# Attention block of 16 batches on one core: transposes two steps, value products six steps behind the scores

## The chip, the cores and the metric

One core of a Trainium2 chip. The time is the device time of one execution in microseconds; less is better. The program is written engine by engine: TensorE (matmuls and transposes into PSUM), VectorE, ScalarE, GpSimd, and a DMA queue issued by SyncE. The engines run their own instruction lists in order and meet only at semaphores.

## The reference, cut to what matters

```python
x = x + attn(xn) + ffn(xn)          # x: (16, 512, 128), xn = layernorm(x)

# attn, 16 heads of 64:
q = einsum('bse,hde->bhsd', xn, Wq) + bq ; k, v the same way
scores = q k^T / 8, causal (later keys masked)
att = softmax(scores) / 8
z = einsum('bhst,bhtd->bhsd', att, v) ; z.reshape(b, s, h * dh) @ proj

# ffn: base product, and of four low-rank experts the one that a router picks
base = xn @ W.T
lw = softmax(l2norm(xn @ Wp.T + bp) @ l2norm(sim) * scale)
res = top-1 weight * (xn @ Wd_e.T) @ Wu_e.T
```

## The kernel before

**Steps.** A batch is 32 steps: 8 pairs of heads times 4 blocks of 128 queries. Step s works on pair s // 4 and on query block s % 4, for both heads of the pair. Since the scores are causal, query block i needs i + 1 blocks of keys: 128, 256, 384 or 512 columns (`width`). The steps of all batches follow each other in one long row; a stage with a lag of n works, at step s, on the unit of step s - n (`due`).

**What a unit goes through.** TensorE makes the scores of both heads (`score`; for blocks 0 and 1 `narrow_scores`, both heads in one bank). VectorE adds the mask, scales and takes the row maximum (`maximum`, line 982). ScalarE takes the exponential and the row sum (`exponentials`, line 721). VectorE takes the reciprocals of the sums (`reciprocals`, line 971), one step late. GpSimd multiplies the probabilities by them (`normalise`, line 632). LAG_T = 3 steps behind the scores TensorE transposes the probabilities block by block (`transpose`, line 1297) into ptp; ScalarE copies head 0's, VectorE head 1's to pt (`evacuate_pt`, lines 732 and 994). Nine steps behind the first scores of a pair (LAG_PV) TensorE multiplies with the values, both heads (`values`, line 1323, 64 columns wide, 32 matmuls). ScalarE makes z_hi from the result one step later, VectorE z_lo = z - z_hi two steps later (`low_z`, line 1000). Eight pairs' results go through the output projection in quarters of six matmuls (`project`, line 1335) at the steps of LAG_OUT.

**Jobs.** Between the transposes and the values TensorE does one job of three 512-column matmuls in most steps (the table JOBS): the queries of a later pair at every step with s % 4 = 3, the keys at every one with s % 4 = 0, value blocks at V_STEPS, the router's product at 1, the transposed expert inputs (`gated`) at 17, the transposes of the next batch's normalised rows (`xt`) at 25. Jobs alternate between the banks jobp0 and jobp1, and a job waits until the job before it in its bank is read out. ScalarE makes the high part of a q or k job (and reads out v jobs), VectorE the low part (q_lo line 870, k_lo line 866); the list `evacuated(s)` says at which step. GpSimd copies k_lo twice to k_low (`pad_low_keys`, line 571) behind its products of the same step, SyncE moves q and k parts by DMA.

**Others.** The router runs in small VectorE instructions at STEP_SUMS to STEP_PARTS, with GpSimd's products (`usq`, `uprod`, at STEP_PRODUCTS) and a power at STEP_UNORM. The layer norm of the next batch is spread over the STEPS_STATS to STEP_SCALE steps. The base and low-rank matmuls stand at step 24, the sum's evacuation, transposes and final addition at 20 and 21.

## Time and profile before

| | us |
|---|---|
| median of 3 runs | 1348.27 (1347.8 to 1348.32) |
| the profiled execution | 1347.42 |
| its span | 1345.7 |
| TensorE matmuls busy | 1330.3 |
| TensorE weight loads busy | 1131.7 |
| VectorE busy | 1106.3 |
| ScalarE busy | 1085.9 |
| GpSimd busy | 997.7 |

The span is the time from the first to the last instruction of the core; the time of a run is that of the whole execution. Matmuls are pipelined, so that a matmul's row is longer than the distance to the next one: the distances between starts are what TensorE needs. Line numbers are those of the kernel before. From one batch to the next the same work starts 82.4 us later.

### The profile page before, as it was taken

Reading aid. Unit: us, or ns where it says so; the run is one execution under the profiler, and the core shown is the slowest. Engines: PE = TensorE matmul, PEld = TensorE weight load, DVE = VectorE, ACT = ScalarE, POOL = GpSimd, SP = SyncE. Lnnn points to the kernel's source line nnn. Section 1 sums busy time; section 2 is a strip of 40 time slices with the busy share of each in tenths; the row PEclk is TensorE's granted clock in tenths of the full one; section 3 lists DMA queues with packets and bytes.
Section 4 is the critical chain, followed back from the end, with each engine's and each line's share of the span. In section 5 each row is a group of like instructions: output and inputs, shape, how many; then the busy total and the mean of one; then the engine's idle time right before and its main releaser. Section 6 shows DMA issues by size and latency. Waiting matters only on the chain.

```text
span 1345.7 us, 34453 instructions
## 1 busy us (share of the span) xinstructions
PE 1330.3 (99%) x10783; PEld 1131.7 (84%) x10783; DVE 1106.3 (82%) x4001; ACT 1085.9 (81%) x3162; POOL 997.7 (74%) x1443
## 2 busy tenths in 40 slices
PE   7999999999999999999999999999999999999998
PEld 5788888888888888888888888888888888888887
DVE  8978888788787878878788787888878888788785
ACT  6887887888788887887888788788888887888785
POOL 7887777778777777777777768777677876778664
PEclk9999999999999999999999999999999999999999
DMA  6455444544544445454444544454454454545541
GB/s 155 95 119 118 103 112 113 122 104 111 125 107 116 105 113 123 103 122 110 116 103 115 123 103 115 112 122 110 103 124 113 103 122 112 122 95 119 118 103 48
DMA packets 112561, 150.59 MB, mean 112 GB/s; under 512 B 18239, under 2 KB 47230, under 8 KB 112382
## 3 DMA queue, kind: packets, MB, share of 16 engines
q1 hardware_dynamic: 111086, 147.97, 46.8%
q8 instruction: 90, 1.47, 0.5%
q14 instruction: 89, 0.73, 0.2%
q10 hardware_dynamic: 1296, 0.42, 0.2%
HBM read 10.69 MB, written 4.19 MB: 11 GB/s over the span
## 4 chain that ended last, share of the span: by engine, by line
PE 95%; ACT 1%; SPq 0%; POOL 0%; DVE 0%; DMA 0%; issue 0%; DVEq 0%; POOLq 0%
PE zp L1323 22%; PE ptp L1297 20%; PE jobp L1167 13%; PE scores L1285 9%; PE scores L1288 7%; PE outp L1335 7%; PE jobp L1172 6%; PE scores L1266 4%; PE scores L1263 3%; PE jobp L1182 1%; PE outp L1344 1%; PE jobp L1187 1%; PE jobp L1360 0%; PE jobp L1177 0%; ACT prob L721 0%; PE outp L1349 0%
## 5 line engine op out<-in xcount | busy, mean ns | idle before, releaser
L632 POOL TENSOR_TENSOR prob<-prob,rden 128x128 f32<-128x128 f32 (+3 forms) x1024 | 712.4, 720 | 247.2 <-DVE rden L971 240.7
L982 DVE CUSTOM_DVE_ANT_0 prob<-scores,mask 128x128 f32<-128x128 f32 (+3 forms) x1024 | 471.7, 488 | 199.8 <-issue 133.3
L721 ACT ACTIVATE prob<-prob,nmax 128x128 f32<-128x128 f32 (+3 forms) x1024 | 567.5, 559 | 12.1 <-DVE nmax L982 5.4
L1297 PE MATMUL ptp<-ident,prob 128*128 128x128 f32 x2560 | 366.9, 274 | 2.1 <-ACT pt L732 1.5
L1297 PEld LDWEIGHTS ptp<-ident,prob 128*128 128x128 f32 x2560 | 295.0, 140 | 27.4 <-POOL prob L632 5.0
L1323 PE MATMUL zp<-pt,v_sb 128*64 128x64 f32 (+3 forms) x4096 | 307.7, 303 | 0.0
L732 ACT ACTIVATE pt<-ptp 128x128 f32<-128x128 f32 (+3 forms) x512 | 221.2, 432 | 102.8 <-PE ptp L1297 102.8
L1323 PEld LDWEIGHTS zp<-pt,v_sb 128*64 128x64 f32 x4096 | 221.6, 137 | 51.2 <-issue 19.7
L994 DVE COPY pt<-ptp 128x128 f32<-128x128 f32 (+3 forms) x512 | 243.3, 475 | 3.9 <-PE ptp L1297 3.1
L571 POOL CAST k_low<-k_lo 64x512 fp32r<-64x512 f32 x256 | 156.0, 609 | 78.0 <-DVE k_lo L866 68.1
L1285 PE MATMUL scores<-k_twice,q_parts 128*128 128x384 f32 (+1 forms) x512 | 200.9, 392 | 0.0
L721 ACT ACTIVATION_READ_ACCUMULATOR prob<-prob,nmax 128x1 f32 x1024 | 198.3, 194 | 0.0
L1288 PE MATMUL scores<-k_low,q_parts 128*128 128x384 f32 (+1 forms) x512 | 186.8, 365 | 0.0
L710 ACT ACTIVATE z_hi<-zp 128x512 fp32r<-128x512 f32 x128 | 76.5, 598 | 127.4 <-PE zp L1323 125.4
L1285 PEld LDWEIGHTS scores<-k_twice,q_parts 128*128 128x128 f32 x512 | 95.9, 187 | 53.6 <-issue 42.7
L1288 PEld LDWEIGHTS scores<-k_low,q_parts 128*128 128x128 f32 x512 | 96.4, 188 | 9.8
L1266 PEld LDWEIGHTS scores<-k_twice,q_parts 128*128 128x128 f32 x512 | 87.5, 188 | 12.4
L870 DVE SCALAR_TENSOR_TENSOR q_lo<-jobp,bqk,q_hi 128x512 fp32r<-128x512 f32 x128 | 95.4, 745 | 1.1 <-ACT q_hi L702 0.2
L866 DVE SCALAR_TENSOR_TENSOR k_lo<-jobp,bqk,k_hi 128x512 fp32r<-128x512 f32 x128 | 95.0, 743 | 0.3 <-ACT k_hi L699 0.3
L1266 PE MATMUL scores<-k_twice,q_parts 128*128 128x128 f32 (+1 forms) x512 | 93.2, 263 | 0.0
L1263 PE MATMUL scores<-k_low,q_hi 128*128 128x256 f32 (+1 forms) x256 | 87.3, 341 | 1.7 <-issue 0.7
L1000 DVE TENSOR_TENSOR z_lo<-zp,z_hi 128x512 fp32r<-128x512 f32 x128 | 87.6, 684 | 0.0
(192 smaller groups left out, 2003.3 us busy)
## 6 DMA issues: line engine op xcount, KB each, us to landing
k_twice<-k_hi SPq DMA_DIRECT2D x506, 128.0 KB, 2.3
q_parts<-q_lo SPq DMA_DIRECT2D x256, 128.0 KB, 2.4
q_parts<-q_hi SPq DMA_DIRECT2D x254, 128.0 KB, 2.3
xin<-in_L_attn_x_dram SPq DMA_DIRECT2D x16, 256.0 KB, 3.1
xres<-in_L_attn_x_dram SPq DMA_DIRECT2D x16, 256.0 KB, 3.1
out_dram<-osb SPq DMA_DIRECT2D x15, 256.0 KB, 2.6
pt<-in_L_attn_Wq_dram SPq DMA_DIRECT2D x1, 512.0 KB, 4.8
pt<-in_L_attn_Wk_dram SPq DMA_DIRECT2D x1, 512.0 KB, 5.6
```

The costliest lines, as they stand in the source:

```text
L571: nc.gpsimd.tensor_copy(k_low[own(h), h, n % 2, :], k_lo[own(h), :].bitcast(F32))\
L632: nc.gpsimd.tensor_tensor(part, part, scale, ALU.mult).then_inc(pn_ready, 1)
L721: nc.scalar.activation(part, part, ACT.Exp, bias=nmax[:, s % NROT, h:h + 1], scale=-1.0, accum_out=den[:, s % NROT, h:h + 1]).then_inc(p_r ...
L732: nc.scalar.activation(pt[:, p % 2, 0, 0:i + 1, P * i:P * i + P], src, ACT.Copy)\
L982: nc.vector.tensor_tensor_reduce(out=prob[:, s % NROT, h, 0:cols], in0=scores[bank][:, first_col:first_col + cols], in1=mask[:, S - cols:S ...
L994: nc.vector.tensor_copy(pt[:, p % 2, 1, 0:i + 1, P * i:P * i + P], src).then_inc(pt_ready[1], 1)
L1167: done = nc.tensor.matmul(dst[:], a[w][:, cols], m[:], start=a is w_hi and m is high, stop=a is w_lo)
L1266: nc.tensor.matmul(scores[i][:, cols * h:cols * h + cols], q_parts[:, h, p % 2, queries], k_twice[:, h, p % 2, 0:cols], start=False, stop= ...
L1285: nc.tensor.matmul(scores[h][:, 0:width(s)], q_parts[:, h, p % 2, queries], k_twice[:, h, p % 2, 0:width(s)], start=True, stop=False)
L1288: nc.tensor.matmul(scores[h][:, 0:width(s)], q_parts[:, h, p % 2, queries], k_low[:, h, p % 2, 0:width(s)], start=False, stop=True).then_i ...
L1297: done = nc.tensor.transpose(ptp[h][:, P * j:P * j + P], prob[:, s % NROT, h, P * j:P * j + P], ident[:])
L1323: done = nc.tensor.matmul(zp[DH * odd:DH * odd + DH, z0 + P // 2 * j:z0 + S // 2], v_sb[:, j, col:col + DH], seen, start=j == NBLK - 1, st ...
```

## The change

The transposes come two steps behind the scores, the values six behind the pair's first (step 2 of the next pair, straight behind its scores and ahead of its transposes), the quarters of the projection go to steps with s % 4 = 1 ahead of the transposes (one stays at 19). VectorE takes both maxima first in every step. The reciprocals of step s - 1 follow at steps with s % 4 of 0, 1 and 2; where s % 4 = 2 those of the same step come too, at its end behind the copy to pt, and at s % 4 = 3 none. k_lo moves from the end of s % 4 = 1 to the middle of s % 4 = 2, GpSimd's k_low copies from step s % 4 = 0 to behind the products of s % 4 = 1. The value job of step 22 goes to step 5, straight behind that step's scores. Some router and layer-norm steps move by one to four.

```diff
-LAG_T = 3
-LAG_PV = (9, 9)
-LAG_Z, LAG_LOW_Z = 10, 11
-LAG_OUT = ((27, 31, 35, 39), (25, 27, 31, 35))
+LAG_T = 2
+LAG_PV = 6
+LAG_Z, LAG_LOW_Z = 7, 7
+LAG_OUT = ((25, 29, 33, 37), (25, 29, 33, 35))
...
-V_STEPS = (29, 30, 2, 6, 10, 14, 18, 22)
+V_STEPS = (29, 30, 2, 5, 6, 10, 14, 18)
...
-STEPS_STATS, STEP_AGGR, STEP_VAR = (5, 9), 17, 17
-STEP_RSTD, STEP_CENTRE, STEP_SCALE = 18, 19, 21
+STEPS_STATS, STEP_AGGR, STEP_VAR = (2, 6), 18, 18
+STEP_RSTD, STEP_CENTRE, STEP_SCALE = 19, 20, 22
...
-STEP_PRODUCTS, STEP_UNORM, STEP_EXPERTS = 3, 4, 7
+STEP_PRODUCTS, STEP_UNORM, STEP_EXPERTS = 2, 6, 10
...
-STEP_SUMS, STEP_LOGITS, STEP_WEIGHTS, STEP_FIRST, STEP_PARTS = 5, 6, 9, 10, 13
+STEP_SUMS, STEP_LOGITS, STEP_WEIGHTS, STEP_FIRST, STEP_PARTS = 6, 9, 10, 14, 14
...
+def subtracted(s):
+
+    if s % NBLK == 2:
+        return [s - 2]
+    return [] if s % NBLK == 3 else [s if s % NBLK == 1 else s - 1]
...
                     normalise(c, s)
-                    if s in JOBS and JOBS[s][0] == "k" and not (last and s in AHEAD):
-                        pad_low_keys(c, s)
+                    if s % NBLK == 1 and not (last and s - 1 in AHEAD):
+                        pad_low_keys(c, s - 1)
...
+                if s == V_STEPS[3]:
+                    job(c, s)
                 unit = due(s, LAG_T, 1, first, tail)
-                if unit is not None:
+                products = s % NBLK == 2
+                if unit is not None and not products:
                     evacuate_pt(c, unit)
                 if s == STEP_EVAC and not first:
                     evacuate_sum(c)
                 if not tail:
                     exponentials(c, s)
+                if unit is not None and products:
+                    evacuate_pt(c, unit)
...
-                between = s % NBLK == NBLK - 1
-                maximum(c, s, 0)
-                if between:
-                    follow()
-                maximum(c, s, 1)
+                for h in range(2):
+                    maximum(c, s, h)
+                unit = due(s, 1, 1, first, tail)
+                if unit is not None and s % NBLK != 3:
+                    reciprocals(c, unit)
+                products = s % NBLK == 2
+                if products:
+                    jobs(c, s, last)
                 router_early(c, s)
-                if not between:
-                    follow()
+                unit = due(s, LAG_T, 1, first, tail)
+                if unit is not None:
+                    evacuate_pt(c, unit)
+                if products:
+                    reciprocals(c, s)
                 p = due(s, LAG_LOW_Z, NBLK, first, tail)
...
+                if not tail and s == V_STEPS[3]:
+                    job(c, s)
+                if s % NBLK == 1:
+                    quarters(c, s, first, tail)
+                p = due(s, LAG_PV, NBLK, first, tail)
+                if p is not None:
+                    for h in range(2):
+                        values(c, p, h)
                 unit = due(s, LAG_T, 1, first, tail)
                 if first and unit == 0:
                     pe.wait_ge(w_lo_ready, 5)
                 if unit is not None:
                     transpose(c, unit)
```

TensorE, step 1 of a pair, from its scores (256 columns a head, two heads in one bank) on. Before: six transposed blocks (step 2's of the pair ahead), then the values (zp).

```order
L1263 MATMUL scores<-k_low,q_hi 128x512
L1266 MATMUL scores<-k_twice,q_parts 128x256 x2
L1297 MATMUL ptp<-ident,prob 128x128 x6
L1323 MATMUL zp<-pt,v_sb 64x64 x2
L1323 MATMUL zp<-pt,v_sb 64x128 x2
L1323 MATMUL zp<-pt,v_sb 64x192 x2
L1323 MATMUL zp<-pt,v_sb 64x256 x2
```

TensorE, the same place after the change, from the last three projection matmuls (outp) that follow these scores. The eight blocks are step 3's of the pair ahead.

```order
L1346 MATMUL outp<-z_hi,proj_hi 128x256
L1346 MATMUL outp<-z_lo,proj_hi 128x256
L1346 MATMUL outp<-z_hi,proj_lo 128x256
L1308 MATMUL ptp<-ident,prob 128x128 x8
L1296 MATMUL scores<-k_twice,q_parts 128x384
L1299 MATMUL scores<-k_low,q_parts 128x384
L1296 MATMUL scores<-k_twice,q_parts 128x384
L1299 MATMUL scores<-k_low,q_parts 128x384
L1334 MATMUL zp<-pt,v_sb 64x64 x2
```

The projection moved ahead of the transposes, step 3's transposes moved here from step 2, and the values moved behind the scores of step 2.

VectorE, step 3 and the start of the next pair's step 0, before (the instruction that only writes nmax reads out the maximum; ISA is the maximum of line 982).

```order
L982 ISA prob,nmax<-scores,mask 128x512
L982 ISA nmax 128x1
L971 RECIPROCAL rden<-den 128x2
L994 COPY pt<-ptp 128x128
L982 ISA prob,nmax<-scores,mask 128x512
L982 ISA nmax 128x1
L1000 TENSOR_TENSOR z_lo<-zp,z_hi 128x8x64
L982 ISA prob,nmax<-scores,mask 128x128
L982 ISA nmax 128x1
L982 ISA prob,nmax<-scores,mask 128x128
L982 ISA nmax 128x1
L971 RECIPROCAL rden<-den 128x2
```

VectorE, the same place after.

```order
L993 ISA prob,nmax<-scores,mask 128x512
L993 ISA nmax 128x1
L993 ISA prob,nmax<-scores,mask 128x512
L993 ISA nmax 128x1
L1005 COPY pt<-ptp 128x2x128
L1011 TENSOR_TENSOR z_lo<-zp,z_hi 128x8x64
L993 ISA prob,nmax<-scores,mask 128x128
L993 ISA nmax 128x1
L993 ISA prob,nmax<-scores,mask 128x128
L993 ISA nmax 128x1
L982 RECIPROCAL rden<-den 128x2
```

Step 2's reciprocal has left step 3 (it now ends step 2), and the copy is that of step 1's two blocks instead of step 0's one. The last row is step 3's reciprocal in both.

GpSimd, the first steps of a batch, before: products of step 2, the router's products, products of step 3, clamp and power, products of step 0, pads.

```order
L632 TENSOR_TENSOR prob<-prob,rden 128x384 x2
L651 TENSOR_TENSOR usq<-u 128x128
L652 TENSOR_TENSOR uprod<-u,simn 128x512
L632 TENSOR_TENSOR prob<-prob,rden 128x512 x2
L642 TENSOR_SCALAR unorm<-unorm 128x4
L645 TENSOR_TENSOR unorm<-unorm,power 128x4
L632 TENSOR_TENSOR prob<-prob,rden 128x128 x2
L571 CAST k_low<-k_lo 64x512 x2
```

GpSimd, the same place after, from step 1's products on.

```order
L639 TENSOR_TENSOR prob<-prob,rden 128x256 x2
L578 CAST k_low<-k_lo 64x512 x2
L658 TENSOR_TENSOR usq<-u 128x128
L659 TENSOR_TENSOR uprod<-u,simn 128x512
L639 TENSOR_TENSOR prob<-prob,rden 128x384 x2
L639 TENSOR_TENSOR prob<-prob,rden 128x512 x2
```

The pads now stand between the products of steps 1 and 2, and in the first pair the router's products behind them.

## Rows read from the trace of the kernel before

**Rows 1.** Busy time by engine, one stretch; then granted clock, DMA share, GB/s.

```profile
core 0: us, PE busy (x) PEld busy (x) DVE busy (x) ACT busy (x) POOL busy (x), PEclk, DMA share, GB/s
...
600.00:680.00 80.00, 80.00 (x660) 68.37 (x658) 66.44 (x243) 65.49 (x192) 60.29 (x86) 1.00 0.48 113
```

**Rows 2.** Waits of TensorE's matmuls: us in total, times, longest.

```profile
PE ptp L1297 <- POOL prob L632: 0.2, 1, 0.2
```

**Rows 3.** Timeline of TensorE, one pair: start, length, what [idle before].

```profile
541.03 0.40 PE L1263 MATMUL scores<-k_low,q_hi 128*128 128x512 f32 x1
...
541.50 0.82 PE L1297 MATMUL ptp<-ident,prob 128*128 128x128 f32 x6
542.25 2.40 PE L1323 MATMUL zp<-pt,v_sb 128*64 128x64 f32 x32
544.58 0.44 PE L1285 MATMUL scores<-k_twice,q_parts 128*128 128x384 f32 x1
...
546.95 0.40 PE L1285 MATMUL scores<-k_twice,q_parts 128*128 128x512 f32 x1
...
547.88 0.38 PE L1297 MATMUL ptp<-ident,prob 128*128 128x128 f32 x2
548.02 0.48 PE L1167 MATMUL jobp<-xq_hi,w_hi 128*128 128x512 f32 x1
...
548.80 0.28 PE L1335 MATMUL outp<-z_hi,proj_hi 128*128 128x256 f32 x1
...
549.51 0.28 PE L1263 MATMUL scores<-k_low,q_hi 128*128 128x256 f32 x1
...
549.80 0.62 PE L1297 MATMUL ptp<-ident,prob 128*128 128x128 f32 x4
550.18 0.47 PE L1167 MATMUL jobp<-xt_hi,w_hi 128*128 128x512 f32 x1
```

**Rows 4.** Timeline of VectorE, the same pair.

```profile
540.93 0.40 DVE L994 COPY pt<-ptp 128x256 f32<-128x256 f32 x1
...
545.33 0.56 DVE L982 CUSTOM_DVE_ANT_0 prob<-scores,mask 128x384 f32<-128x384 f32 x1
...
547.70 0.69 DVE L982 CUSTOM_DVE_ANT_0 prob<-scores,mask 128x512 f32<-128x512 f32 x1 [0.55 <-PE scores L1288]
...
549.19 0.69 DVE L1000 TENSOR_TENSOR z_lo<-zp,z_hi 128x512 fp32r<-128x512 f32 x1
550.10 0.29 DVE L982 CUSTOM_DVE_ANT_0 prob<-scores,mask 128x128 f32<-128x128 f32 x1 [0.22 <-issue]
```

**Rows 5.** Timeline of ScalarE, end of step 3's exponentials.

```profile
549.94 0.19 ACT L721 ACTIVATION_READ_ACCUMULATOR prob<-prob,nmax 128x1 f32 x1
```

**Rows 6.** Timeline of GpSimd, the same pair.

```profile
545.44 1.28 POOL L571 CAST k_low<-k_lo 64x512 fp32r<-64x512 f32 x2 [1.60 <-DVE k_lo L866]
546.80 1.18 POOL L632 TENSOR_TENSOR prob<-prob,rden 128x256 f32<-128x256 f32 x2
548.56 1.61 POOL L632 TENSOR_TENSOR prob<-prob,rden 128x384 f32<-128x384 f32 x2 [0.57 <-DVE rden L971]
550.77 1.04 POOL L632 TENSOR_TENSOR prob<-prob,rden 128x512 f32<-128x512 f32 x1 [0.60 <-DVE rden L971]
```

**Rows 7.** Timeline of all engines in the first batch, a wait for GpSimd.

```profile
67.35 1.01 POOL L529 TENSOR_TENSOR rstd<-var_eps,power 128x4 f32<-128x4 f32 x1
...
67.44 0.55 PE L1297 MATMUL ptp<-ident,prob 128*128 128x128 f32 x3 [0.23 <-POOL prob L632]
```

**Rows 8.** Timeline of VectorE: first of the router's last group, instruction behind the group.

```profile
543.13 0.39 DVE L1061 TENSOR_TENSOR lg<-lg 128x16 f32<-128x16 f32 x1
...
544.57 0.74 DVE L866 SCALAR_TENSOR_TENSOR k_lo<-jobp,bqk,k_hi 128x512 fp32r<-128x512 f32 x1
```

**Rows 9.** GpSimd's groups of instructions by line: busy us, mean ns | idle before.

```profile
L652 POOL TENSOR_TENSOR uprod<-u,simn 128x512 f32<-128x512 f32 x16 | 20.7, 1296 | 0.0
L645 POOL TENSOR_TENSOR unorm<-unorm,power 128x4 f32<-128x4 f32 x16 | 16.6, 1037 | 1.3
```

**Rows 10.** Timeline of GpSimd at xt_lo, step 25.

```profile
576.68 1.29 POOL L623 TENSOR_TENSOR xt_lo<-xt,xt_hi 128x512 fp32r<-128x512 f32 x1
```

More of the change, by code:

```diff
@@ L1099, in step @@
                     job(c, UNITS - 1, back=1)
-                for js in evacuated(s):
-                    if js in JOBS and not (last and js in AHEAD):
-                        job(c, js)
+                if not products:
+                    jobs(c, s, last)
                 for half, due_step in enumerate(FIRST_STATS if first else STEPS_STATS):
```

48 lines of the change are left out of this document (19 added, 29 removed).

## The prediction

> **What bounds the kernel now.** I read first the busy times of one stretch in the middle [rows 1]: TensorE is busy for the whole 80 us, at the full granted clock of 2.4 GHz, and no other engine for over 67 us. Then TensorE's own list of waits [rows 2]: over the whole run the normalised probabilities (GpSimd, line 632) held its matmuls up once, for 0.2 us. Then one pair of heads in TensorE's timeline [rows 3]: scores, transposes, job, scores, transposes, values, each starting where the one ahead lets it. The kernel before is bound by the length of TensorE's own stream. Whatever the other engines do, they do behind it, and the question is only whether the change leaves them there.
>
> I number the steps of a pair 0 to 3 (step s of a batch is step s mod 4; it has s mod 4 + 1 blocks of 128 columns) and count from t, the start of step 3's scores. The profiled execution took 1347.4 us with a span of 1345.7; the median of the three runs is 1348.3, within 0.1% of it. The sum goes on 1347.4.
>
> **Work on TensorE: nothing changes.** Each matmul is still there, and the kinds that follow each other differ at one edge only. Today the values start 0.75 us after the start of six transposed blocks and the scores behind them start 2.33 us after the values [rows 3]. In the new order they are entered from scores and left to two transposed blocks. No row shows that edge. Between full-width work and the half-width values the array drains for about 0.1 us and the first weight load after it is uncovered for another 0.1 (an estimate from those rows: six blocks at the 0.12 that four take each would need 0.6 to 0.7, and the first of the 384-column scores behind the values takes longer than the others). Both edges together are at most 0.2 us a pair, so over 128 pairs the new edge is worth between -26 and +26 us. I take 0, since there are two such edges before and after.
>
> **Transposes two steps behind: the chain that must fit.** For the widest step, 3, the way from its scores to its transposes is, on TensorE after the change [rows 3]: scores 0.93 (546.95 to 547.88), four blocks 0.38 (549.80 to 550.18), job q 0.78 (548.02 to 548.80), narrow scores 0.29, six blocks 0.59 (0.38 and two more), job k 0.78, scores of step 1 0.47, six projection matmuls 0.71, and the four blocks of head 0, 0.44: TensorE comes to head 1's transposes of step 3 at t + 5.37.
>
> The other side: VectorE starts the maxima at t + 0.75 (547.70 against 546.95) and is through two of them, 0.69 each less the 0.07 by which its instructions overlap, at t + 1.98. Then it copies step 1's transposes (0.40 less 0.07), then makes z_lo (0.69 less 0.07), so it is free at t + 2.93. Step 0's scores start at t + 2.09 (0.93 + 0.38 + 0.78) and their first maximum 0.59 later (550.10 against 549.51), which would be t + 2.68: the engine, not the scores, is late. Two maxima of 0.29 less 0.07 follow, and only then the reciprocal, at t + 3.37 [rows 3, 4]. The exponentials end at t + 3.18 (549.94 + 0.19) [rows 5] and don't decide. GpSimd starts 0.67 after the first of these maxima (550.77 against 550.10), 0.23 of it behind the reciprocal, and needs twice 1.04 [rows 4, 6]: t + 5.68. Where a matmul of before did wait for GpSimd, in the first batch, it started 0.09 after GpSimd's next instruction [rows 7]: t + 5.77 against 5.37. **A wait of 0.4 us** in every pair in which nothing else sits between. In the kernel before TensorE came a step later and nothing of this was seen. The bounds: 0.15, if VectorE were through before the scores come (0.25 less), and 0.7, if ScalarE came last, which now has a wider block to evacuate ahead of these exponentials.
>
> **Where that wait shows in a batch.** Steps 1, 13 and 17: 0.4 each. At 5 a value job (0.77) now stands ahead; no wait there, but that job itself needs bank 1 back, that is q_lo, which VectorE makes behind the copy of step 4: 0.3. At 21 there are no projection matmuls: 0.4 + 0.7 = 1.1. At 25 base and low-rank matmuls (0.93) stand in between: none. At 9 and 29 a wait for step 2's transposes (next) has taken it. At 13 and 17 VectorE comes late to the maxima, since the router's small instructions now sit behind the reciprocal at the end of third steps: the group at step 14 takes 1.44 (543.13 to 544.57) [rows 8]. The reciprocal it follows waits, on its engine, for step 2's own transposes behind the values: s2 + 0.87 + 2.33 + 0.2 to head 1's block, then 0.5 for hand-over and copy, so s2 + 3.95 (an estimate: the copy's row has a wider block), and the next maxima could start at s2 + 4.96. Room 1.0, so 0.5 more at 17; at 10 the group has as many links but no wide one, and I take 1.2, 0.25 more at 13. Sum of this part: 0.4 + 0.3 + 1.1 + 0.65 + 0.9 = 3.35 us.
>
> **GpSimd's queue, step 2's transposes.** From step 2's scores (s2) the new order is: maxima from s2 + 0.75 (545.33 against 544.58), 0.14 later where the wait above has pushed step 3's copy into them, 0.56 less 0.07 each [rows 4], reciprocal of step 1 at s2 + 1.87, GpSimd 0.23 behind it, products of step 1 1.18, the two pads of k_low 1.28 (they stood ahead of step 1's products before), products of step 2 1.61 [rows 6]: done at s2 + 6.2. TensorE wants head 1 at s2 + 6.8 (step 2: scores and drain 0.87, values 2.33, two blocks with the drain 0.24, job 0.78 [rows 3]; step 3: 2.09; then 0.29 and three blocks). Room 0.6. Into this room fall:
> at step 2 uprod (1.30) [rows 9] and usq, a quarter of its size (0.4 at most): with the router's two VectorE copies that gives 0.9 at step 4;
> at step 6 the power, 1.04 [rows 9], and the clamp ahead of it (some 0.2): 0.5 at step 8;
> at step 9 the logits (0.9 on VectorE ahead of step 10's maxima): 0.25 at step 12, of which the 13th step gives none back;
> at step 25 the three evacuations of xt, which ScalarE can only do behind the exponentials, and those now stand behind the evacuation of step 23's transposes, which come after the projections; xt_lo (1.29) [rows 10] then starts at 7.5 us after step 24's scores and step 25's products at 8.9 instead of some 6.5. Step 26 has no job to cover it: 0.6 at step 27 and, with the pads in between, 1.3 at step 28: 1.9.
> Sum: 0.9 + 0.5 + 0.25 + 1.9 = 3.55 us. The bound below is 0 for each, if the power and xt_lo overlap with waits; above, 1.5 times.
>
> **Value products six steps behind, later router steps.** They move TensorE work earlier and buffers free earlier; nothing waited for them, so nothing is gained. At the start the pipe fills sooner (up to 2 us less), at the end step 31's chain is as long as before with one block of values less beside it (up to 2 us more): 0.
>
> **The sum.** 3.35 + 3.55 = 6.9 us a batch, on a batch of 82.4. The first batch is partly limited otherwise and the last, without the jobs for a next one, waits more; 15 batches in full and no more: 103 us. 1347.4 + 103 = **1450 us**.
>
> **A rule that speaks for the change.** In rows 1 the weight loads fill 68.4 of 80 us, 85%, while the matmuls fill all. The Trainium skill, page "Perfetto Trace Analysis", section "Identifying the Most-Contended Engine", holds matmul busy time to be no good measure of TensorE's headroom and takes the busy share of weight loads instead. By it 15% of the time, some 200 us, is slack that a better order could reach. Here the row speaks against: four 512-column matmuls take 0.93 us, 0.23 each, back to back [rows 3], and the loads' gaps lie at the values and under wide matmuls.
>
> **The rivals.**
> (A) Forecast, waits of 3 to 9 us a batch: 1390 to 1490, 64%.
> (B) Only the reciprocal chain counts and GpSimd's room is larger than I find: under 3 us a batch, 1352 to 1390, 20%. For it: my slack of 0.6 has errors of the size of the terms.
> (C) No wait at all, TensorE's stream as before: 1346 to 1351, 5%. It needs every one of the 0.4 and 0.9 to be wrong. That the change doesn't do what it says falls here too; the instruction order excludes most of it.
> (D) Faster: no waits, and the values' new edge to the transposes saves its drain and uncovered load, 0.2 x 128 = 26 us: down to 1322. It decides if TensorE's first transposes follow the values within 0.22 us, as values follow values, and the step-3 wait is under 0.2 us. 6%. The rule above is a part of it.
> (E) The waits feed each other (late evacuations delay the next scores): over 1490, 5%.
>
> Measured differences under 0.2% (2.7 us) can't be told from none. Faster: D, 6%. Same: C, 5%. Slower: the rest, 89%. The range leaves out D, C, the lower edge of B and the upper edge of A with E: 1368 to 1488.
>
> **What would show it.** TensorE busy 92 to 94% of the span in the middle; in its list of waits the transposes waiting for GpSimd's prob at the top, some 100 us in all, with single ones of 0.3 to 1.2; step-3 reciprocals 3.36 us after their scores; a batch of 89 us. The prediction is wrong if TensorE's stretches stay at 100%, or if most of the idle time ends on scores (maxima late) or on pt copies.

## The result, and the profile after

| | before | after |
|---|---|---|
| median | 1348.2 us (1347.8 to 1348.3) | 1482.9 us (1481.9 to 1483.7) |
| ratio | | 1.100, 95% interval 1.099 to 1.102 |
| span of the profiled execution | 1345.7 | 1480.1 |
| one batch in the middle | 82.4 | 90.7 |
| TensorE's waits for prob, matmuls and weight loads | 21, 5.2 us | 431, 165.5 us |

The changed kernel is 134.7 us slower; 1450 was predicted, in a range from 1368 to 1488. The span's part of it, 134.4 us, lies at 8.30 in each of the 14 batches between the first and the last (116.2), 12.3 in the first (90.9 against 78.6), 5.8 in the last (101.3 against 95.5 from its first scores to the end) and 0.2 ahead of the first.

The stretch that answers to [rows 1], busy time by engine, then granted clock, DMA share and GB/s:

```profile
core 0: us, PE busy (x) PEld busy (x) DVE busy (x) ACT busy (x) POOL busy (x), PEclk, DMA share, GB/s
600.00:680.00 80.00, 75.67 (x590) 60.95 (x589) 60.08 (x211) 60.89 (x173) 55.33 (x79) 1.00 0.44 104
```

TensorE has 4.3 us without a matmul in 80 and does 590 where it did 660, at the same full clock; every other engine is less busy in the stretch than before. TensorE waits, and more than the 4.3 us say: the row of a matmul is longer than its distance to the next one, so the first part of a wait still counts as busy. Over the whole run TensorE's busy time rises by 57 us (1387.8 against 1330.3) with the same work, and its idle time by 77 us only. For what it waits, the list of waits says (us in total, times, longest), which answers to [rows 2]:

```profile
engine line waited for: us in total, times, longest us
POOL prob L639 <- DVE rden L982: 394.4, 247, 2.9
DVE pt L1005 <- PE ptp L1308: 237.9, 277, 2.4
ACT pt L739 <- PE ptp L1308: 204.4, 307, 1.7
PEld ptp L1308 <- POOL prob L639: 123.5, 284, 1.3
...
PEld scores L1274 <- issue: 45.6, 63, 1.5
...
PE ptp L1308 <- POOL prob L639: 42.0, 147, 1.2
...
PE scores L1274 <- DVE nmax L993: 19.6, 27, 1.1
DVE stats L841 <- DMA xin<-in_L_attn_x_dram: 19.1, 14, 2.1
```

The transposes wait for GpSimd's prob, on the weight load where the operand is needed first and on the matmul. But there is a second kind that the prediction doesn't have: narrow scores (line 1274) that wait for a bank, which VectorE's maxima of the step before read out too late. To put a size to each I took, for the twelve batches that follow the first two, the time from start to start of TensorE's instructions, less what the same pair of neighbours takes when nothing is waited for, by step (us a batch):

| step | predicted | transposes for prob | scores for maxima |
|---|---|---|---|
| 1 | 0.4 | 0.42 | |
| 4 | 0.9 | 0.56 | 0.50 |
| 5 | 0.3 | 0.14 (the job) | |
| 8 | 0.5 | 0.87 | |
| 12 | 0.25 | 0.23 | 0.06 |
| 13 | 0.65 | 0.51 | |
| 16 | - | 0.24 | 1.13 |
| 17 | 0.9 | 0.51 | |
| 21 | 1.1 | 0.85 | |
| 24 | - | 0.16 | |
| 27 and 28 | 1.9 | 1.50 | 0.49 |
| sum | 6.9 | 5.99 | 2.18 |

Together 8.17 of the 8.30 us a batch. Steps 9, 25 and 29, for which no wait was predicted, have none. TensorE's stream itself is longer by at most 0.2.

**The chain of step 3, as it ran.** TensorE, from the first scores of a step 3 (t = 651.24) to the transposes of its second head, which answers to [rows 3]; start, length, what, [idle before]:

```profile
651.24 0.39 PE L1296 MATMUL scores<-k_twice,q_parts 128*128 128x512 f32 x1
...
654.94 0.40 PE L1274 MATMUL scores<-k_low,q_hi 128*128 128x512 f32 x1
...
656.12 0.60 PE L1308 MATMUL ptp<-ident,prob 128*128 128x128 f32 x4
656.90 0.66 PE L1308 MATMUL ptp<-ident,prob 128*128 128x128 f32 x4 [0.19 <-POOL prob L639]
```

VectorE in the same time, and GpSimd, which answer to [rows 4, 6]:

```profile
651.99 0.69 DVE L993 CUSTOM_DVE_ANT_0 prob<-scores,mask 128x512 f32<-128x512 f32 x1 [0.88 <-issue]
...
653.22 0.42 DVE L1005 COPY pt<-ptp 128x256 f32<-128x256 f32 x1
653.55 0.68 DVE L1011 TENSOR_TENSOR z_lo<-zp,z_hi 128x512 fp32r<-128x512 f32 x1
654.15 0.28 DVE L993 CUSTOM_DVE_ANT_0 prob<-scores,mask 128x128 f32<-128x128 f32 x1
...
654.57 0.16 DVE L982 RECIPROCAL rden<-den 128x2 f32<-128x2 f32 x1
```

```profile
654.81 2.40 POOL L639 TENSOR_TENSOR prob<-prob,rden 128x512 f32<-128x512 f32 x3 [1.60 <-DVE rden L982]
```

The reciprocal starts at t + 3.33 (3.37 predicted), GpSimd 0.24 behind it (0.23), and the second head's transposes at t + 5.66 (5.77), 0.78 after the first head's, which take 0.4. A wait of 0.4, as predicted.

**The late maxima.** VectorE at the end of step 14 and the start of step 15, whose scores start at 695.81, then GpSimd in the same time, and the narrow scores of step 16 on TensorE:

```profile
695.31 0.29 DVE L1005 COPY pt<-ptp 128x128 f32<-128x128 f32 x1 [0.39 <-PE ptp L1308]
695.52 0.15 DVE L982 RECIPROCAL rden<-den 128x2 f32<-128x2 f32 x1
695.59 0.15 DVE L1072 TENSOR_TENSOR lg<-lg 128x16 f32<-128x16 f32 x1
695.78 0.60 DVE L1074 TENSOR_TENSOR gated<-dn,lg 128x128 f32<-128x128 f32 x1
696.41 0.88 DVE L1079 CAST gated_parts<-gated 128x256 fp32r<-128x256 f32 x1
697.32 0.80 DVE L1082 TENSOR_TENSOR gated_parts<-gated,gated_parts 128x128 fp32r<-128x128 f32 x1
698.04 0.68 DVE L993 CUSTOM_DVE_ANT_0 prob<-scores,mask 128x512 f32<-128x512 f32 x1
```

```profile
696.31 1.66 POOL L639 TENSOR_TENSOR prob<-prob,rden 128x384 f32<-128x384 f32 x2
```

```profile
698.88 0.35 PE L1274 MATMUL scores<-k_low,q_hi 128*128 128x256 f32 x1 [0.87 <-DVE nmax L993]
```

VectorE may not go on to step 14's last work before TensorE has made the transposes behind the values (copy at 695.31). Then the router's group stands in its queue, and step 15's maxima start 2.23 us behind their scores, where 0.75 is usual. TensorE waits 0.87 for the bank. The group takes 2.45 us (695.59 to 698.04), where the same four instructions took 1.44 in the kernel before [rows 8], and 1.30 in most of its other batches: there the last two took 0.29 us each, in every batch but the first, with GpSimd idle; here they take 0.88 and 0.80, in every batch. GpSimd now makes step 14's products beside them, 0.83 us a head, and both end 0.15 us after one of its two products.

### The profile page after: what moved, and what is told of

It reads as the page before. It is cut to its first block and busy times, and to the rows that moved or that the text cites. A ratio compares the mean times of both kernels' runs of the same rounds, so it can differ in the third digit from the quotient of the medians.

```text
span 1480.1 us, 34437 instructions
## 1 busy us (share of the span) xinstructions
PE 1387.8 (94%) x10783; PEld 1117.2 (75%) x10783; DVE 1119.2 (76%) x4001; ACT 1113.7 (75%) x3162; POOL 997.9 (67%) x1443
## 3 DMA queue, kind: packets, MB, share of 16 engines
q8 instruction: 90, 1.47, 0.4%
## 5 line engine op out<-in xcount | busy, mean ns | idle before, releaser
L993 DVE CUSTOM_DVE_ANT_0 prob<-scores,mask 128x128 f32<-128x128 f32 (+3 forms) x1024 | 459.8, 486 | 59.0 <-issue 42.9
L1308 PE MATMUL ptp<-ident,prob 128*128 128x128 f32 x2560 | 410.6, 281 | 51.4 <-POOL prob L639 42.0
L1005 DVE COPY pt<-ptp 128x128 f32<-128x128 f32 (+3 forms) x512 | 249.2, 487 | 238.0 <-PE ptp L1308 237.9
L1308 PEld LDWEIGHTS ptp<-ident,prob 128*128 128x128 f32 x2560 | 280.7, 140 | 169.3 <-POOL prob L639 123.5
L728 ACT ACTIVATION_READ_ACCUMULATOR prob<-prob,nmax 128x1 f32 x1024 | 194.9, 190 | 0.0
L1274 PE MATMUL scores<-k_low,q_hi 128*128 128x256 f32 (+1 forms) x256 | 91.1, 356 | 23.5 <-DVE nmax L993 19.6
L706 ACT ACTIVATE k_hi<-jobp,bqk 128x512 fp32r<-128x512 f32 x128 | 87.1, 681 | 3.9 <-PE jobp L1178 3.6
L1274 PEld LDWEIGHTS scores<-k_low,q_hi 128*128 128x128 f32 x256 | 48.0, 187 | 53.6 <-issue 45.6
```

What stands on the lines that cost most here:

```text
L728: nc.scalar.activation(part, part, ACT.Exp, bias=nmax[:, s % NROT, h:h + 1], scale=-1.0, accum_out=den[:, s % NROT, h:h + 1]).then_inc(p_r ...
L993: nc.vector.tensor_tensor_reduce(out=prob[:, s % NROT, h, 0:cols], in0=scores[bank][:, first_col:first_col + cols], in1=mask[:, S - cols:S ...
L1005: nc.vector.tensor_copy(pt[:, p % 2, 1, 0:i + 1, P * i:P * i + P], src).then_inc(pt_ready[1], 1)
L1274: nc.tensor.matmul(scores[i][:, 0:2 * cols].rearrange("p (h k) -> p h k", k=cols), q_hi[:, p % 2, queries], k_low[:, :, p % 2, 0:cols], st ...
L1308: done = nc.tensor.transpose(ptp[h][:, P * j:P * j + P], prob[:, s % NROT, h, P * j:P * j + P], ident[:])
```

## The experiments

Every time is a median of four runs against a kernel before of 1348.0 to 1348.1 in the same series; intervals are of the ratio, 95%.

**1. The lag of the transposes alone.** b_t2, the kernel before with

```diff
-LAG_T = 3
+LAG_T = 2
```

> The kernel before with one number changed: the transposes stand two steps behind the scores instead of three. Values, projection, VectorE's order of work and the router steps stay as before. Theory (the waits come from the lag of the transposes: the softmax chain of a step, maximum, exponentials, reciprocal, two products on GpSimd, no longer fits between the scores and the transposes): here TensorE comes to the third step's second head even earlier than in the changed kernel, at t + 4.7 us instead of t + 5.4, since the projection matmuls of step 1 stand behind the transposes, and the chain ends at t + 5.8 as there: a wait of about 1.1 us per pair of heads, 8 to 11 us per batch, 1480 to 1520 us. Rival (the order of TensorE's stream, the values ahead of the transposes and six steps behind, costs the time): nothing of it is in this kernel, 1348 us. Rival (VectorE's new order and the router's new steps cost it): 1348 to 1360 us as well.

Measured: 1540.8 us, ratio 1.143 (1.141 to 1.145): one number, slower than the whole change. Its waits:

```profile
POOL prob L632 <- DVE rden L970: 319.7, 270, 4.2
...
PEld ptp L1295 <- POOL prob L632: 219.3, 514, 2.1
...
PE ptp L1295 <- POOL prob L632: 64.5, 187, 1.9
```

The transposes of a step 3's unit wait 0.85 us in step 1 of most pairs, where 1.1 was expected, and those of a step 1's unit 0.36 in step 3, for which nothing was; with larger ones at steps 5 and 24 it is 10.6 a batch. The lag of two is enough by itself, and the whole change costs 58 us less than it. The projection matmuls and the values that now stand ahead of the transposes fit that, but no run has them alone with a lag of two.

**2. The new order of values and transposes alone.** b_vfirst, the kernel before with, in TensorE's step,

```diff
+                for h in range(2):
+                    p = due(s, LAG_PV[h], NBLK, first, tail)
+                    if p is not None:
+                        values(c, p, h)
                 unit = due(s, LAG_T, 1, first, tail)
...
-                for h in range(2):
-                    p = due(s, LAG_PV[h], NBLK, first, tail)
-                    if p is not None:
-                        values(c, p, h)
```

> The kernel before with the values (still nine steps behind) ahead of the transposes within their step, the edge scores to values to transposes of the changed kernel, alone. Theory (the edges cost what they cost before): 1345 to 1351 us. Rival (the new edge saves its drain and uncovered load, 0.2 us in each of 128 pairs): 1322 us. Rival (it costs as much more): 1374 us. If a wait for prob shows up, it isn't from the edge, since the transposes come later, not earlier.

Measured: 1431.8 us, 1.062 (1.061 to 1.064): none of the three. The edge is free: the pairs in which nothing is waited for, the first and the last of a batch, take 10.76 and 10.63 us, against 10.76 and 10.61 in the kernel before. The time is waits, of kinds that the kernel before has hardly any of (1.3 us for the maxima, none of TensorE's for k_lo):

```profile
POOL k_low L571 <- DVE k_lo L866: 293.2, 124, 3.7
...
PEld scores L1285 <- DVE nmax L982: 65.5, 123, 2.1
...
PE jobp L1172 <- DVE k_lo L866: 13.8, 17, 1.0
```

There are also 46.6 us of weight loads that wait for prob (5.0 before). VectorE's copy of a transposed block now waits until the values (2.3 us) are through, and behind the copy stand k_lo and the next maxima. A value job waits 1.04 us for k_lo at step 14, scores 0.67 and 1.62 us for maxima at steps 19 and 27. That the values stand first costs through VectorE's queue, not through TensorE's edges, and it needs no lag of two. This is so in VectorE's old order; the changed kernel makes k_lo ahead of the copy, and no run has the order of its values apart from the rest.

**3. The changed kernel with the transposes three steps behind, the values seven.** a_t3:

```diff
-LAG_T = 2
-LAG_PV = 6
-LAG_Z, LAG_LOW_Z = 7, 7
+LAG_T = 3
+LAG_PV = 7
+LAG_Z, LAG_LOW_Z = 8, 8
```

> The changed kernel with the transposes three steps behind the scores again; the values follow at seven steps (six isn't possible then), z_hi and z_lo at eight. Everything else is the changed kernel's: values ahead of transposes, VectorE's order, pads, router and statistics steps. Theory (the lag of two is the cause): the transposes' waits for prob go, some 5.7 us a batch; what stays are the narrow scores that wait for late maxima (2.1 us a batch in the changed kernel, from the statistics' wait for the load of x and the router groups), part of it: 1352 to 1385 us. Rival (TensorE's new edges and order): stays at 1470 to 1483 us. Rival (VectorE's order and the router's steps are the cause): stays above 1430 us.

Measured: 1548.8 us, 1.148 (1.145 to 1.151). All three theories fail, since the run changed a second thing: the values moved from third steps to fourth steps.

```profile
POOL prob L639 <- DVE rden L984: 466.9, 322, 3.9
...
PEld jobp L1187 <- DVE k_lo L879: 103.1, 95, 1.9
...
PE jobp L1187 <- DVE k_lo L879: 80.4, 95, 1.6
...
PEld ptp L1312 <- POOL prob L639: 21.2, 63, 0.7
```

The waits for prob fall to 21.2 us on the weight loads, as the theory has it, and the value jobs of third steps wait for k_lo in their place: 0.98, 1.00, 1.35, 0.91, 1.26 and 0.97 us at steps 2, 6, 10, 14, 18 and 30. VectorE makes k_lo at a third step behind its maxima. That it was the values of the same step that gave it the time is borne out by run 4, where the values are back there and the waits for k_lo fall from 103.1 to 2.9 us on weight loads and from 80.4 to 2.4 on matmuls.

**4. The same with the values at third steps.** a_t3v10: LAG_T = 3, LAG_PV = 10, LAG_Z, LAG_LOW_Z = 11, 11.

> The changed kernel with the transposes three steps behind and the values ten (z_hi, z_lo eleven), so that the values stand where the change has them, at third steps ahead of transposes and job. The run with the values at seven steps moved them to fourth steps, where they no longer cover k_lo for the value jobs, and its waits were of another kind (value jobs waiting for k_lo, 0.9 to 1.35 us each, five times a batch). Theory (the lag of two is the cause in the changed kernel): the waits for prob go and nothing takes their place but late maxima: 1350 to 1380 us. Rival (values ahead of the transposes delay what stands behind the transposes' copies on VectorE whatever the lag): value jobs or scores wait again, 1400 to 1440 us, as the kernel before with the values first did (1432).

Measured: 1447.9 us, 1.074 (1.073 to 1.076). Expected were 1350 to 1380.

```profile
PEld scores L1278 <- issue: 75.6, 64, 2.2
PE scores L1278 <- DVE nmax L995: 47.4, 46, 1.7
...
PEld ptp L1312 <- POOL prob L639: 32.2, 85, 0.7
```

The lag's own waits are gone, a step 3's prob is ready 3.3 us and more ahead of its transposes, and the time falls by 35 us only. The kind that I had left out of the prediction has grown: narrow scores wait 0.98, 1.31 and 1.24 us at steps 4, 12 and 16, behind statistics and router groups that stand on third steps (2, 10, 14), where VectorE makes the step's own reciprocal 4.95 us after the scores.

**5. The same, with the groups' steps as before.** a_t3steps: run 4 with the lines below; the steps of the deviation, the centring and the final addition go back with them.

```diff
-STEPS_STATS, STEP_AGGR, STEP_VAR = (2, 6), 18, 18
+STEPS_STATS, STEP_AGGR, STEP_VAR = (5, 9), 17, 17
...
-STEP_PRODUCTS, STEP_UNORM, STEP_EXPERTS = 2, 6, 10
+STEP_PRODUCTS, STEP_UNORM, STEP_EXPERTS = 3, 4, 7
...
-STEP_SUMS, STEP_LOGITS, STEP_WEIGHTS, STEP_FIRST, STEP_PARTS = 6, 9, 10, 14, 14
+STEP_SUMS, STEP_LOGITS, STEP_WEIGHTS, STEP_FIRST, STEP_PARTS = 5, 6, 9, 10, 13
```

> The run with transposes three and values ten steps behind (1448), with the steps of router, statistics and the next batch's centring as in the kernel before: no group at a third step but the logits' at 6. In that run the narrow scores of steps 4, 12 and 16 waited 0.98, 1.31 and 1.24 us for maxima that VectorE came late to, behind what it does at the end of third steps after the reciprocal that waits for the copy. Theory (VectorE's third steps are full: the reciprocal there is 4.95 us after its scores, and each group behind it goes on to the next scores): 3.5 to 4.5 us a batch less, 1375 to 1395 us; the logits' group, now at step 6, makes one new wait at step 8. Rival (the fixed order, the reciprocal behind the copy, costs it without any group): it stays above 1430 us.

Measured: 1381.3 us, 1.025 (1.023 to 1.026), 66.6 less than run 4. The waits at steps 4, 12 and 16 fall from 3.5 to nothing, and step 8 has a new one, 0.26 for the scores and 0.21 at the transposes, as expected. Of what stays, 33 us, waits explain 1.3 us a batch (the rest of it at steps 27 and 28, the next batch's xt, 0.54); the other 0.7 a batch isn't settled.

**6. The changed kernel, lags as they are, with the groups' steps as before.** a_steps: the same lines on the changed kernel.

> The changed kernel (lags 2 and 6) with the steps of router, statistics and centring as in the kernel before. Theory (two causes that cover each other: the chain that is too long for two steps, and the groups on full third steps; where one wait goes, the other shows): a small gain, as the last groups alone gave 11 us: 1460 to 1478 us. Rival (the groups are the greater cause at this lag too, 4 us a batch as with three steps): 1410 to 1425 us. Rival (GpSimd's queue of step 2 decides and now has usq and uprod ahead of step 3's products instead): the wait goes from step 4 to step 5 and the time stays at 1480 us.

Measured: 1469.1 us, 1.090 (1.088 to 1.091), 13.8 less than the changed kernel. Runs 4 to 6 and the changed kernel make a square, each cause with and without the other (us):

| | groups as before | groups as changed | difference |
|---|---|---|---|
| transposes 3, values 10 behind | 1381.3 | 1447.9 | 66.6 |
| transposes 2, values 6 behind | 1469.1 | 1482.9 | 13.8 |
| difference | 87.8 | 35.0 | |

If the two causes added up, the differences of both rows would be the same; as it is, 53 us of one lie over the other: a wait of one kind takes up time in which the other would have been seen. What was 0.56 and 0.50 at step 4 and 0.87 at step 8 is now 0 and 0, and 1.40 at step 24 (0.16 before), 0.80 at the job of step 10 and 0.40 at step 9 have come: waits for prob stay at the top.

```profile
PEld ptp L1308 <- POOL prob L639: 119.6, 276, 2.3
PE ptp L1308 <- POOL prob L639: 41.5, 117, 2.1
```

**7. The kernel before with the changed groups' steps.** b_steps: the lines of run 5 the other way round, on the kernel before.

> The kernel before with nothing changed but the steps of router, statistics and centring, which are the changed kernel's (groups at steps 2, 6, 9, 10 and 14). Theory (the groups cost only where VectorE's third steps are full, that is with the reciprocal that waits there for the copy behind the values; in the kernel before the copies are due before the values and VectorE has room): 1348 to 1356 us. Rival (these steps cost by themselves, as late maxima of steps 3, 11 and 15): 1380 to 1410 us.

Measured: 1385.6 us, 1.028 (1.026 to 1.029). The theory falls, the rival holds: these steps cost 37.5 us in the old order too.

```profile
PE ptp L1297 <- ACT pt L732: 16.4, 48, 0.5
...
PE scores L1263 <- DVE nmax L982: 5.8, 11, 1.0
```

Maxima start 2.00, 1.47 and 1.87 us after the scores of steps 3, 11 and 15 instead of 0.76. Narrow scores wait for them (0.40 at step 4, 0.23 at 16), and ScalarE, whose exponentials follow the maxima, copies head 0's transposes late (0.53, 0.40 and 0.59 at steps 5, 13 and 17).

**8. Single sources of late maxima in the changed kernel.** a_stats moves the statistics, which wait 19.1 us for the load of x:

```diff
-STEPS_STATS, STEP_AGGR, STEP_VAR = (2, 6), 18, 18
+STEPS_STATS, STEP_AGGR, STEP_VAR = (5, 9), 18, 18
```

> The changed kernel with the two halves of the statistics of the next batch's x at steps 5 and 9, as before the change, instead of 2 and 6. In the changed kernel VectorE waits for the load of x at step 2 in 14 batches, 19.1 us in all, and the maxima of step 3 start 1.6 us after their scores instead of 0.75, so that the narrow scores of step 4 wait 0.44 us and its transposes 0.56. Theory (late maxima are the second cause beside the lag, and the load of x is one source of them): 0.5 to 1.0 us a batch less, 1467 to 1475 us. Rival (TensorE waits for GpSimd there anyway, so the load costs nothing): 1481 to 1484 us.

Measured: 1489.0 us, 1.105 (1.103 to 1.106), 6 more, so neither. The narrow scores of step 4 no longer wait, and its transposes wait 1.00 instead of 0.56; those of step 8, behind the statistics' new place, 1.26 instead of 0.87. a_parts moves the router's last groups off step 14:

```diff
-STEP_SUMS, STEP_LOGITS, STEP_WEIGHTS, STEP_FIRST, STEP_PARTS = 6, 9, 10, 14, 14
+STEP_SUMS, STEP_LOGITS, STEP_WEIGHTS, STEP_FIRST, STEP_PARTS = 6, 9, 10, 11, 13
```

> The changed kernel with the router's last two groups at steps 11 and 13 instead of both at 14. In the changed kernel the maxima of step 15 start 2.25 us after their scores, the narrow scores of step 16 wait 1.1 us for them, and the transposes at steps 16 and 17 wait 0.24 and 0.51 for prob. Theory A (such waits add up; I left this one out of the sum): 1.1 to 1.6 us a batch less, 1457 to 1466 us. Theory B (what the run with the later statistics suggests: where a wait of the scores goes, the transposes wait for prob instead, since the softmax chain counts from the scores): 0 to 0.5 us a batch less, 1474 to 1483 us.

Measured: 1471.6 us, 1.092 (1.090 to 1.094), 11.3 less, between the two theories. Gone are 1.13 at step 16's scores and 0.33 at step 17; come are 0.29 at step 12's transposes and 0.36 at the job of step 14. Of 1.46 us a batch 0.7 are kept. The new waits stand just behind the steps to which the groups went. In a_stats it is another thing: at step 4 itself the wait for maxima (0.50) goes and the wait for prob grows by 0.44, so that a late maximum costs there only what it is longer than the wait that would stand in its place.

**9. A link of the chain.** a_zlo8: z_lo one step later.

```diff
-LAG_Z, LAG_LOW_Z = 7, 7
+LAG_Z, LAG_LOW_Z = 7, 8
```

> The changed kernel with z_lo made at first steps instead of fourth steps. The prediction's chain has z_lo (0.62 us of VectorE) between step 3's maxima and step 0's, and with it the engine, not the scores, is late for step 0's maxima, by 0.25 us, and so is the reciprocal of step 3. Theory (chain as predicted): the waits of the transposes at steps 1, 13, 17 and 21 (0.42, 0.51, 0.51, 0.67) and at 5 shrink by 0.25 each, since the scores then set the maxima: about 1.3 us a batch less, 1462 us. Rival (ScalarE's exponentials, now behind a wider block, are last): no change, 1480 to 1485 us. Third way: z_lo now stands ahead of step 1's maxima and takes as much there: 1485 to 1495 us.

Measured: 1482.1 us, 1.100 (1.098 to 1.101): no change. Yet the link is where the prediction put it: the waits at steps 1, 13 and 17 shrink from 0.42, 0.51 and 0.51 to 0.25, 0.23 and 0.23, and the maxima of step 0 start 0.59 instead of 0.88 after their scores. What is won there is given back elsewhere, at step 4 (the scores' wait goes from 0.50 to 0.87, the transposes' from 0.56 to 0.44) and at the job of step 5 (0.14 to 0.59): z_lo now stands ahead of step 1's maxima, which start at 1.26 instead of 0.85 after their scores.

**10. The pads' place.** a_pads: k_lo at second steps and its two pads ahead of the second step's products, as before the change.

```diff
-    if s % NBLK == 2:
-        return [s - 2]
-    return [] if s % NBLK == 3 else [s if s % NBLK == 1 else s - 1]
+    return evacuated(s)
...
-                scaled = 0 if setup else c.fixed(c.head(s + 1, 1))
+                scaled = 0 if setup else c.fixed(c.head(s, 1))
...
-                    if s % NBLK == 1 and not (last and s - 1 in AHEAD):
-                        pad_low_keys(c, s - 1)
+                    if s in JOBS and JOBS[s][0] == "k" and not (last and s in AHEAD):
+                        pad_low_keys(c, s)
```

> The changed kernel with k_lo on VectorE and its two pads on GpSimd where the kernel before has them: k_lo at second steps, behind the copy of the transposes; pads ahead of the second step's products. Theory (the two pads, 1.28 us, only change place within GpSimd's queue ahead of the third step's products, whose end stays): the waits at steps 4, 8, 12, 24, 27 and 28 stay, and since k_lo would stand behind a copy that itself waits for late transposes, the pads wait: 1480 to 1520 us. Rival (the pads' new place makes the third steps' products late, 2.8 us a batch): 1438 us.

Measured: 1478.3 us, 1.096 (1.095 to 1.098), 4.6 less. The rival falls; the expected loss does not come either. GpSimd waits 189.8 us for k_lo, and 141.7 us less for rden. TensorE's waits do not stay where they were, as the theory had it: step 28 loses 1.5 us a batch, step 8 0.4 and step 24 0.2, while the scores of step 12 gain 0.94, those of step 27 0.3 and the transposes of steps 23 and 29 0.35 each. The sum stays, its parts don't.

```profile
POOL prob L637 <- DVE rden L980: 252.7, 193, 3.2
...
POOL k_low L576 <- DVE k_lo L875: 189.8, 126, 2.4
```

**11. The chain without most of GpSimd's work.** a_norm128: the products on the first 128 columns only.

```diff
-                    part = prob[:, s % NROT, h, 0:width(s)]
-                    scale = rden[:, s % NROT, h:h + 1].to_broadcast([P, width(s)])
+                    part = prob[:, s % NROT, h, 0:P]
+                    scale = rden[:, s % NROT, h:h + 1].to_broadcast([P, P])
```

> The changed kernel with GpSimd's products made of the first 128 columns of each head only, whatever the step's width: the other columns of the probabilities stay unscaled, so that much of the normalisation is left out. The wait for the reciprocal and the hand-over stay; GpSimd's part of the chain falls from 2.08 us to some 0.8 at fourth steps, from 1.6 to 0.8 at third steps. Theory (the transposes' waits for prob are the chain's last link and GpSimd's queue): the 5.7 us a batch of waits for prob go, the 2.1 us of narrow scores that wait for maxima stay: 1385 to 1400 us. Rival (TensorE's waits circulate: VectorE, which waits for the transposes' copies, sets the pair, and a shorter GpSimd only moves the wait to the scores): 1430 to 1470 us.

Measured: 1394.2 us, 1.034 (1.033 to 1.036). Its busy times, and its waits:

```profile
PE 1354.9 (97%) x10783; PEld 1118.7 (80%) x10783; DVE 1085.1 (78%) x4001; ACT 1108.1 (79%) x3162; POOL 675.0 (48%) x1443
```

```profile
POOL prob L639 <- DVE rden L982: 637.9, 398, 3.4
...
PEld ptp L1308 <- POOL prob L639: 38.2, 86, 0.7
```

GpSimd is busy for 323 us less and waits for the reciprocals 243.5 us more; a batch in the middle is 5.0 us shorter, and 88.7 us of the run are back. Not all of it is the predicted mechanism, a lag of two with a chain that ends in 2.1 us of products: the transposes wait some 4.4 us a batch less, but the scores wait 0.9 less too, since step 16's wait for maxima (1.13) is gone; the router's group ahead of them is held up less by the shorter products (last section). The mechanism's part is thus some 70 us. Of what remains, 3.3 us a batch in the middle, 1.24 are scores that wait for maxima (1.04 of it at step 4), some 1.4 transposes that still wait for prob (0.49 at step 27).

## Why the prediction was right, and where its sum was short

- **The bound of the kernel before.** Right. By the same count by step its stream has no wait in a middle batch (the 5.0 us of weight loads that waited for prob over the run don't show there). The edits of three runs (1, 2 and 7) and the change itself made it wait; none of the twelve runs is faster than the kernel before.
- **Work on TensorE, 0 within 26 us.** Right: the stream is longer by at most 0.2 us a batch, and run 2 shows the new edge alone at 0.02 us a pair. Rival D, faster by it, had nothing to win. What the order does elsewhere stands in this part at nothing: the values ahead of the transposes hold VectorE's copies back. With VectorE's old order that is 84 us (run 2). The prediction has this delay in step 2's reciprocal alone; what it costs in the changed kernel no run shows by itself.
- **The chain of step 3.** Right in each of its links within 0.1 us, by the rows above and by run 9. Of step 2's reciprocal the prediction's own terms add up to 3.90 us after the scores, not 3.95; it ran at 3.90.
- **Where it shows in a batch, 3.35.** Measured 2.43 at the same steps (0.42 + 0.14 + 0.51 + 0.51 + 0.85). Steps 13 and 17 were given 0.25 and 0.5 for the router's groups at the transposes; they show 0.1 each. The groups' lateness comes out one step earlier, as a wait of step 16's scores (1.13), and once TensorE waits there, the chain of step 16 counts from scores that are late already. At 21 the missing projection matmuls were added in full (1.1 for 0.85).
- **GpSimd's queue, 3.55.** Measured 3.16 at steps 4, 8, 12, 27 and 28; step 8 undersized (0.87 for 0.5), step 4 oversized by as much (0.56 for 0.9). Steps 16 and 24 show another 0.40 that had no term. In run 10 the place of k_lo and its pads is worth 4.6 us net, though single steps change by up to 1.5.
- **What had no term: scores that wait for maxima, 2.18 us a batch.** This is the step that failed. I followed a late maximum to prob, and not to the bank that it reads out. I also gave the group at step 14 its 1.44 us of the kernel before [rows 8]; it takes 2.45, beside GpSimd's products, and that is the difference between maxima that are 0.5 late, as worked out for step 17, and the 1.5 measured. In run 8, a_parts, with the group at step 13, its three wide instructions take 0.29 each. And the statistics, moved to step 2, were costed at nothing: VectorE waits there up to 2.1 us for the load of x: in the kernel before, with the first half at step 5, no such wait is in its list. Moving them back alone gains nothing, though (run 8).
- **15 batches in full.** 6.9 x 15 = 103.5. The 14 in the middle bring 1.4 each more (19.6), the first and the last 18.1 together instead of 6.9 (11.2). That the first batch has 12.3 and the last 5.8 fits work which shorter lags pull forward out of the last into the first; no run tells that apart.
- **How near the sum came, and luck in it.** It was short by 1.4 us a batch: 2.18 for the scores, 0.40 at steps 16 and 24 and 0.13 of the stream were missing, while the two sums above were 0.92 and 0.39 too large. So 1.3 of the 2.7 us missing were made up by terms that were too large. At steps 4 and 17 (0.73) a wait of the scores, there or one step earlier, took the place of part of the wait for prob. The other 0.6 (steps 5, 13, 21, 27 and 28, less what was missing at 8) have no such reason, and that part of the nearness is luck.
- **The rivals.** B, only the reciprocal chain counts, falls: steps 4, 8, 12, 27 and 28 wait too, and with short products most of those waits go (run 11). C and D, no wait, fall by the time. Of E, waits that feed each other, the runs show the contrary in the changed kernel: they cover each other (the square of runs 4 to 6; run 8, a_stats).
- **What would show it.** TensorE is busy for 75.67 of 80 us in the middle, 95% (92 to 94 predicted), prob is at the top of its waits, and a batch takes 90.7 (89). The busy share says too little of the waits, as shown above: 8.3 us of waiting in a batch of 90.7 are 9%. TensorE's list has 165 us for prob where some 100 were said; the table by step, which counts only by how much the next start is later, has 5.85 a batch without the job of step 5, 94 us.
- **The rule that spoke for the change.** The share of weight loads fell from 68.4 of 80 us [rows 1] to 60.95, from 85% to 76%, and the time rose by 10%. The Trainium skill, page "Perfetto Trace Analysis", section "Identifying the Most-Contended Engine", judges TensorE's headroom by this share, together with the share of its peak arithmetic. For the difference of the two kernels this case's traces agree: the changed kernel has 9 points more headroom, and 9% of its batch is waiting. That the 15% of the kernel before were slack they do not bear out: it had no waits, and no run made it faster, but none was an attempt to.

What stays open: 0.7 us a batch of run 5, why the sum of the waits stays the same in run 10, and what the new order of the values costs in the changed kernel. No version came out faster than the kernel before.

## What to carry to other kernels

When a stage is moved nearer to its producer, write down the chain between them link by link on one clock, as was done here for step 3, and follow each late instruction to everyone who waits for it, to the bank that it frees as well as to the data that it makes. In-order queues turn an order into a wait: work put ahead of something that another engine copies out delays all that stands behind that copy (run 2), so ask of every move what it covered. Waits of two kinds in one loop can cover each other: a single edit that removes one may show little (run 6, and a_stats in run 8), or bring waits at another step (a_parts, runs 9 and 10), and the parts must be measured together before a cause is called small. And a busy share of an engine with overlapping rows says too little of its waits: take the distances between starts.

## What the runs showed of the hardware that was not expected

TensorE's clock fell in the slowest kernel, run 3 (mean 0.992 in the profiled execution), where the profiled executions of all others stayed at 0.998 or above. Six stretches of 2 us of it; the columns are those of [rows 1]:

```profile
278.00:280.00 2.00, 2.00 (x18) 1.97 (x17) 1.16 (x6) 1.69 (x6) 0.78 (x3) 1.00 0.90 206
280.00:282.00 2.00, 0.99 (x9) 0.75 (x7) 0.77 (x2) 1.62 (x5) 0.30 (x1) 1.00 0.89 205
282.00:284.00 2.00, 1.21 (x4) 0.59 (x4) 2.00 (x7) 1.56 (x5) 2.00 (x3) 1.00 0.47 112
284.00:286.00 2.00, 1.72 (x16) 1.39 (x18) 1.48 (x6) 0.23 (x1) 1.80 (x4) 0.62 0.03 8
286.00:288.00 2.00, 2.00 (x20) 1.52 (x16) 0.00 (x0) 0.00 (x0) 1.26 (x2) 0.53 0.00 0
288.00:290.00 2.00, 2.00 (x17) 1.60 (x14) 0.46 (x2) 1.35 (x4) 0.00 (x0) 1.00 0.00 0
```

After two stretches in which TensorE was busy 0.99 and 1.21 of 2 us the granted clock goes to its lower level, 1.2 GHz, for most of the next two (means 0.62 and 0.53), and back to 2.4 GHz; in these two the engine is busy for 1.72 and 2.00 us. At a mean of 0.992 this is some 12 of the 200 us that this kernel is slower, and its four executions bear that out: 1552.0 and 1550.2 us at 0.992, 1547.4 at 0.996, 1540.8 at 0.999. The changed kernel, whose waits for prob are 1.3 us at most, shows no such stretch: in windows of 10 us from 20 to 1470 it stays at 1.00.

Two of VectorE's instructions between tensors in SBUF take up to three times as long beside GpSimd's products: `gated_parts<-gated`, 128 x 256, took 0.29 us beside an idle GpSimd (kernel before, a_parts, b_steps), 0.88 beside its products of 384 columns, and 0.37 beside those cut to 128 columns (run 11). In all 16 batches it ends 0.15 us after a product of GpSimd, which fits waiting rather than slower work. The Trainium skill, page "SBUF — State Buffer", section "SBUF: two separate sides", has the rule: the two engines share a pair of ports under an exclusive lock; an instruction of VectorE with two inputs in SBUF, or in a mode that takes both of its ports, blocks until the GpSimd instruction that came first ends, and the other way round. The trace agrees for these two, of which one has two inputs in SBUF; which mode the other runs in no row shows. So the duration of such an instruction can't be taken from a row alone, only together with what GpSimd does at that place. The router's group takes some 1.1 us a batch more (2.45 against 1.30), 18 us over the run; VectorE's busy time as a whole rose by 12.9.

The hand-over from GpSimd to TensorE, from the end of the product to the transpose that waited for it, is 0.06 us in the mean of 12 batches (the transposes of steps 13, 17 and 21). It is no other in the kernel before: the 0.09 that the prediction read there [rows 7] runs from the start of GpSimd's next instruction, whose row begins 0.04 before the product's ends; from the product's end it is 0.06. The prediction added the 0.09 to an end, and took twice 1.04 us for two products whose rows overlap by 0.04. With GpSimd's start 0.03 earlier than worked out, this is why the second head's transposes came at t + 5.66 and not 5.77.
